# Squared lengths of the context taken from row loads for three batches, x lengths in two halves, last distance store in halves

## The chip, the cores and the metric

One core of one Trainium2 chip runs the whole program. The metric is the device time of one execution in microseconds, as the median over several runs. The engines are TensorE (PE, with its weight loads as PEld), VectorE (DVE), ScalarE (ACT), GpSimd (POOL) and SyncE (SP); DMAs are issued here by SP and ACT.

## The reference, cut to what matters

Eight batches; `x` is 100 rows of 512 numbers per batch, the context `ctx` 722 rows of 512. Four blocks follow one another, each adding to `x`: an alignment of the normalised `x` with the context by dynamic time warping, a mixture of experts, a cross attention and a second feed-forward. The change lies in the first step of the first block, the distances:

```python
aa = jnp.sum(a * a, axis=-1)[:, None]        # a: context, 722 x 512
bb = jnp.sum(b * b, axis=-1)[None, :]        # b: layernorm(x), 100 x 512
D = jnp.sqrt(jnp.maximum(aa + bb - 2.0 * (a @ b.T), 0.0))
```

The warping then walks the 722 x 100 table of D of each batch from one corner to the other and back, so it can't begin before D of all eight batches is in place (this kernel walks the eight tables at once).

## The kernel before, in words

`distances` is the first of the program's stages; `warp` follows after a barrier of all engines. Context rows are dealt to tiles by turns: tile t of the CT = 6 holds rows t, t+6, ..., so that tiles 0 and 1 have 121 rows and the others 120 (WHOLE = 120, MORE = 2, B = 8 batches, S = 100, D = 512, KD = 4, TPT = 3 tiles to a PSUM bank). For each batch b:

- SP (L171 to L182) loads the transposed context into one of four tiles `cT` (L178). From batch 4 on it first waits until the products and the squares of batch b-4 have read the buffer.
- ACT squares it, 2888 numbers per partition (`square`, L301); DVE adds the four blocks to one in two steps (`square_sums`, L239 and L243); PE multiplies the sum with a column of ones, 12 records of matmul with one column (`lengths`, L350); DVE copies the six columns into `aa` (`squares`, L248 and L249). That is `aa` of the reference.
- PE forms the products with the transposed, scaled `x`, 48 records (`products`, L339), into two PSUM banks, two pairs of which take turns.
- DVE adds products, `aa` and `bb`, three tiles after each bank (`squares`, L257); ACT takes Relu (L282) and Sqrt (L288) of all six tiles at once (`roots`).
- ACT issues the store of the distances to DRAM, a large one (L153) and a small one for the rows left over (L155); SP waits for both and loads the table back in the layout of the warping (`load_cost`, L163). `warp` waits for all eight of these loads (semaphore `c_in`), and its DVE loop (L851 to L855) starts then.

The order of the work is written out by hand. PE runs products(0), the transposes of x for batches 4 to 7, lengths(0), two small matmuls for the ranks of the mask (L365, L366), two products that spread `bb` (L370), and then for n = 1 to 7

```python
if n >= AHEAD:      # AHEAD = 6
    lengths(n)
products(n)
if n < AHEAD:
    lengths(n)
```

DVE runs square_sums(n+1) ahead of squares(n) and, after batch 0, `keep_ranks` (L134 to L149), whose positions release POOL's 48 instructions at L218. ACT runs square(n) and then roots(n-3), for n up to 10. SP issues load_cost(b-5) after the cT load of batch b, and the others at the end. The squared length of a row of normalised x (`bb`) is worked out on DVE from mean and variance after all of x (L263 to L266), for all 800 rows at once, and copied from PSUM at L271. Ahead of products(0), PE runs 10 pairs of matmuls (`keep_awake`, L81) whose result nobody reads.

Of the kernel before, what the change touches and what calls it, by code (L numbers as in the profile page):

```python
# [83 lines left out]
def distances(nc, io, res):  # L84

    ctx = ExitStack()
    with ctx:
# [9 lines left out]
        lens = res["Wmem"][0:S, B * D:B * D + B * S].rearrange("p (b s) -> p b s", s=S)  # L97
        bb = sb("bb", [P, B * S])
        NCT = 4
        cT = [sb(f"cT{i}", [P, KD, C]) for i in range(NCT)]  # L100
        cq = [sb(f"cq{i}", [P, KD, C]) for i in range(2)]
        cs = [sb(f"cs{i}", [P, C]) for i in range(2)]
        aa = sb("aa", [P, B * CT])
        d2 = sb("d2", [P, 2, CT, S])
        ds = sb("ds", [P, 2, CT, ST])
        tp = [pb(f"tpa{i}", [P, KD, P]) for i in range(2)]
        pbb = [pb(f"pbb{i}", [P, 512]) for i in range(2)]
# [11 lines left out]
        TPT, AHEAD = 3, 6  # L119
# [6 lines left out]
        prk, ptk = pbb[1][:, 400:400 + CT * B], pbb[1][:, 400 + CT * B:400 + 2 * CT * B]  # L126
# [23 lines left out]

        def store(act, b):
            act.wait_ge(ds_ok, b + 1)
            act.dma_start(res["dist"][b, 0:WHOLE * CT, :].rearrange("(p t) j -> p t j", t=CT),  # L153
                         ds[0:WHOLE, b % 2, :, :]).then_inc(ds_out[b % 2], 16)
            act.dma_start(res["dist"][b:b + 1, WHOLE * CT:C, :], ds[WHOLE:WHOLE + 1, b % 2, 0:MORE, :]).then_inc(ds_out[b % 2], 16)  # L155

        def load_cost(sp, b):

            sp.wait_ge(ds_out[b % 2], 32 * (b // 2 + 1))
            blocks = bass.AP(tensor=res["dist"].tensor, offset=b * CP * ST + PAD, ap=[[BL * ST - SK, NB], [1, BL * ST]])  # L160
            if b == 0:
                sp.wait_ge(below_out, 16)
            sp.dma_start(res["cost_mem"][b * NB:(b + 1) * NB, 0:BL * ST], blocks).then_inc(res["c_in"], 16)  # L163

        @block.sync
        def _(sp):
            for g in range(B // 2):
                sp.dma_start(x_sb[:, 2 * g:2 * g + 2, :], io["x"][2 * g:2 * g + 2].rearrange("b s d -> s b d")).then_inc(x_in[g], 16)
            sp.wait_ge(below_set, 1)
            sp.dma_start(res["dist"][:, C:CP, :].rearrange("b r s -> r b s"), below[:, :, :]).then_inc(below_out, 16)  # L170
            sp.wait_ge(m0, 1)  # L171
# [12 lines left out]
        @block.gpsimd  # L184
# [36 lines left out]
        @block.vector  # L221
        def _(dve):
            link = make_linker(dve, res["dve_chain"])
            dve.memset(d2[:, :, :, :], 0.0).then_inc(zf, 1)
            for g in range(B // 2):
                bs = slice(2 * g, 2 * g + 2)
                dve.wait_ge(x_in[g], 16)
                layernorm_stats(link, dve, x_sb[:, bs, :], stats[:, bs, :], mv[:, bs, :], 2)
                dve.tensor_scalar(rstd[:, bs], mv[:, bs, 1], EPS, None, ALU.add).then_inc(var_ok, 1)
                dve.wait_ge(st_ok, g + 1)  # L230
                link(dve.reciprocal(rstd[:, bs], rstd[:, bs]))
                for b in (2 * g, 2 * g + 1):
                    dve.tensor_scalar(xl[:, b, :], x_sb[:, b, :], mv[:, b, 0:1], rstd[:, b:b + 1],
                                      ALU.subtract, ALU.mult).then_inc(xl_ok, 1)
            def square_sums(b):

                q = cq[b % 2]
                dve.wait_ge(cq_ok, b + 1)
                dve.tensor_tensor(q[:, 0:2, :], q[:, 0:2, :], q[:, 2:4, :], ALU.add).then_inc(half_ok, 1)  # L239
                dve.wait_ge(half_ok, b + 1)  # L240
                if b >= 2:
                    dve.wait_ge(aa_mm, b - 1)
                dve.tensor_tensor(cs[b % 2][:, :], q[:, 0, :], q[:, 1, :], ALU.add).then_inc(cs_ok, 1)  # L243

            def squares(b):

                dve.wait_ge(aa_mm, b + 1)
                dve.tensor_copy(aa[0:WHOLE + 1, b * CT:b * CT + MORE], pa[b % 2][0:WHOLE + 1, 0:MORE])  # L248
                dve.tensor_copy(aa[0:WHOLE, b * CT + MORE:b * CT + CT], pa[b % 2][0:WHOLE, MORE:CT]).then_inc(aa_ok, 1)  # L249
                dve.wait_ge(aa_ok, b + 1)  # L250
# [12 lines left out]
            link(dve.tensor_tensor(length[:, :], rstd[:, :], rstd[:, :], ALU.mult))  # L263
            link(dve.scalar_tensor_tensor(length[:, :], mv[:, :, 1], float(D), length[:, :], ALU.mult, ALU.mult))
            dve.wait_ge(id1, 1)
            dve.tensor_tensor(lens[:, :, :], ident[0:S, 0:S].unsqueeze(1).broadcast_to([S, B, S]),  # L266
                              length[:, :].unsqueeze(2).broadcast_to([S, B, S]), ALU.mult).then_inc(lens_ok, 1)
            square_sums(0)
            for g in range(2):
                dve.wait_ge(bb_mm, g + 1)  # L270
                dve.tensor_copy(bb[:, g * 400:(g + 1) * 400], pbb[g][:, 0:400]).then_inc(bb_ok, 1)  # L271
            dve.wait_ge(bb_ok, 2)
            for n in range(B):
                if n + 1 < B:
                    square_sums(n + 1)
                squares(n)
                if n == 0:
                    keep_ranks(dve, link)

        def roots(act, b):  # L280
            act.wait_ge(d2_ok, 2 * b + 2)
# [10 lines left out]
        def _(act):  # L292
# [16 lines left out]
            square(0)  # L309
            for b in range(B - 4, B):  # L310
                keep_T(b)
            for n in range(1, B + 3):
                if n < B:
                    square(n)
                if n >= 3:
                    roots(act, n - 3)

        @block.tensor
        def _(pe):
# [24 lines left out]
            def lengths(b):  # L344
# [5 lines left out]
                    ins = pe.matmul(pa[b % 2][0:TR[t], t:t + 1], cs[b % 2][:, TO[t]:TO[t] + TR[t]], ones[:, 0:1], start=True, stop=True)  # L350
                ins.then_inc(aa_mm, 1)

            keep_awake(pe, pbb[0], ident, 13)
# [10 lines left out]
            pe.wait_ge(kept_ok, 1)  # L364
            pe.matmul(prk[:, :], lower[:, :], kept[:, :, :].rearrange("p t b -> p (t b)"), start=True, stop=True).then_inc(rk_ok, 1)  # L365
            pe.matmul(ptk[:, :], onesb[:, :], kept[:, :, :].rearrange("p t b -> p (t b)"), start=True, stop=True).then_inc(rk_ok, 1)  # L366
            for g in range(2):
                if g == 0:
                    pe.wait_ge(lens_ok, 1)
                pe.matmul(pbb[g][:, 0:400], ones[0:S, :], lens[:, 4 * g:4 * g + 4, :].rearrange("p b s -> p (b s)"),  # L370
                          start=True, stop=True).then_inc(bb_mm, 1)
# [2228 lines left out]
```

## Time and profile before

| | us |
|---|---|
| median of 3 runs | 1186.57 (1183.56 to 1186.99) |
| the profiled execution | 1183.51 |
| its span in the profile | 1181.6 |
| PE, DVE, ACT, POOL busy | 1065.4, 455.3, 348.5, 216.8 |
| mean granted clock of TensorE | 0.955 |

The span begins with the first instruction and ends with the last; some 1.9 us of the execution's own time lie outside it. The profiled execution is 3.1 us below the median, at the lower end of the runs. The stage of the distances takes the first 83 us. Times in the rows below are microseconds from the start of the span. Granted clock 1.00 is 2.4 GHz and 0.50 is 1.2 GHz.

### The profile page before, as it was taken

Reading aid. Unit: us, or ns where it says so; the run is one execution under the profiler, and the core shown is the slowest. Engines: PE = TensorE matmul, PEld = TensorE weight load, DVE = VectorE, ACT = ScalarE, POOL = GpSimd, SP = SyncE. Lnnn points to the kernel's source line nnn. Section 1 sums busy time; section 2 is a strip of 40 time slices with the busy share of each in tenths; the row PEclk is TensorE's granted clock in tenths of the full one; section 3 lists DMA queues with packets and bytes.
Section 4 is the critical chain, followed back from the end, with each engine's and each line's share of the span. In section 5 each row is a group of like instructions: output and inputs, shape, how many; then the busy total and the mean of one; then the engine's idle time right before and its main releaser. Section 6 shows DMA issues by size and latency. Waiting matters only on the chain. (4 is left out here: it accounts for less than half of the span.)

```text
span 1181.6 us, 17361 instructions
## 1 busy us (share of the span) xinstructions
PE 1065.4 (90%) x5421; PEld 690.2 (58%) x5422; DVE 455.3 (39%) x1694; ACT 348.5 (29%) x827; POOL 216.8 (18%) x340
## 2 busy tenths in 40 slices
PE   8956679955988999999999999989999999999997
PEld 7952235533457677777767777655456655555553
DVE  6828888883572000000000000037865553121212
ACT  4534755771021222222222222234254430000000
POOL 1853031110001111112112121210030001121211
PEclk9978799977898999999999999989999999999999
DMA  8858005117515655865595555570030005000000
GB/s 308 227 117 279 6 1 172 69 55 195 203 43 205 204 183 189 321 191 190 185 332 187 186 187 188 176 210 1 1 143 1 1 1 161 1 0 1 14 14 28
DMA packets 71802, 152.83 MB, mean 129 GB/s; under 512 B 12066, under 2 KB 16298, under 8 KB 70910
## 3 DMA queue, kind: packets, MB, share of 16 engines
q1 hardware_dynamic: 63494, 131.21, 32.7%
q0 software_dynamic: 6928, 17.04, 6.4%
q10 hardware_dynamic: 1320, 3.84, 1.2%
q8 instruction: 29, 0.48, 0.2%
q14 instruction: 31, 0.25, 0.1%
HBM read 131.83 MB, written 20.25 MB: 129 GB/s over the span
## 5 line engine op out<-in xcount | busy, mean ns | idle before, releaser
L1327 ACT ACTIVATE att<-ba,b 128x128 f32<-128x128 f32 x216 | 79.3, 367 | 308.0 <-PE ba L1297 308.0
L1347 DVE TENSOR_TENSOR att<-ba,att 128x512 f32<-128x512 f32 x27 | 18.7, 691 | 368.5 <-PE ba L1305 368.5
L1297 PEld LDWEIGHTS ba<-tiles,shared 128*128 128x128 f32 x896 | 111.5, 192 | 37.4 <-issue 37.4
L1297 PEld LDWEIGHTS ba<-tiles,Wmem 128*128 128x128 f32 x832 | 105.1, 194 | 39.3 <-issue 39.3
L1297 PE MATMUL ba<-tiles,shared 128*128 x896 | 114.4, 276 | 1.2 <-issue 0.3
L1297 PE MATMUL ba<-tiles,Wmem 128*128 x832 | 107.9, 279 | 6.0 <-issue 4.5
L1305 PE MATMUL ba<-shared,att 128*128 128x512 f32 x224 | 110.0, 593 | 0.0
L1305 PE MATMUL ba<-Wmem,att 128*128 128x512 f32 x208 | 102.2, 593 | 0.0
L2416 PE MATMUL acc<-tiles 128*128 128x400 f32 x256 | 90.6, 505 | 0.0
L2482 DVE SCALAR_TENSOR_TENSOR tiles<-bf,shared 128x400 f32<-128x400 f32 x64 | 32.4, 566 | 129.9 <-PE bf L2401 129.6
L2375 PE MATMUL bf<-shared,Wmem 128*128 128x400 f32 x192 | 70.0, 501 | 2.3 <-PEq L49 1.5
L2416 PEld LDWEIGHTS acc<-tiles 128*128 128x128 f32 x256 | 47.1, 190 | 40.4 <-issue 8.6
L1370 POOL DMA_INDIRECT sum_d<-att,to_row x27 | 43.1, 1595 | 145.3 <-DVE att L1350 145.3
L2325 POOL TENSOR_TENSOR tiles<-tiles 128x400 f32<-128x400 f32 x32 | 32.4, 1033 | 153.4 <-DVE tiles L2482 153.4
L2375 PEld LDWEIGHTS bf<-shared,Wmem 128*128 128x128 f32 x192 | 36.1, 190 | 30.1 <-issue 2.2
L2342 ACT COPY outT<-acc 128x400 f32<-128x400 f32 x4 | 1.8, 495 | 172.4 <-PE acc L2416 172.4
L887 DVE TENSOR_TENSOR_SCAN cost_mem<-reach_mem,cost_mem,enter 128x93 bf16<-128x93 bf16 x115 | 47.2, 411 | 12.1 <-DVE cost_mem L880 0.5
L1811 DVE RECIPROCAL shared<-shared 128x400 f32<-128x400 f32 x16 | 42.4, 2652 | 21.0 <-ACT shared L1711 20.8
L1521 PE MATMUL ba<-shared,Wmem 128*128 128x400 f32 x128 | 46.1, 504 | 2.6 <-DVE qT L1814 1.5
L1024 PE MATMUL px<-ctx_rows,cost_mem 128*100 128x512 f32 (+1 forms) x96 | 46.4, 626 | 0.0
L1305 PEld LDWEIGHTS ba<-shared,att 128*128 128x128 f32 x224 | 36.1, 192 | 13.4 <-issue 13.4
L855 DVE TENSOR_TENSOR_SCAN ctx_rows<-ctx_rows,cost_mem 128x46 f32<-128x46 f32 x115 | 37.4, 325 | 12.3 <-DVE ctx_rows L852 0.5
(396 smaller groups left out, 1674.7 us busy)
## 6 DMA issues: line engine op xcount, KB each, us to landing
Wmem<-in_W SPq DMA_DIRECT2D x16, 2048.0 KB, 14.1
shared<-in_W SPq DMA_DIRECT2D x16, 2048.0 KB, 12.2
cT<-in_ctxT SPq DMA_DIRECT2D x8, 1444.0 KB, 10.6
ctx_rows<-in_ctx SPq DMA_DIRECT2D x8, 1280.0 KB
Wmem<-in_Wkv SPq DMA_DIRECT2D x2, 2048.0 KB, 9.2
att<-in_b SPq DMA_DIRECT2D x16, 256.0 KB, 14.1
tiles<-in_WoT SPq DMA_DIRECT2D x4, 1024.0 KB, 13.6
Wmem<-in_WiT SPq DMA_DIRECT2D x3, 1024.0 KB, 7.1
```

The costliest lines, as they stand in the source:

```text
L855: dve.tensor_tensor_scan(reach[:, s + 1, 1:ROW], lower[:, s, :], cost[:, :, s], reach[:, s + 1, 0:1], ALU.min, ALU.add).then_inc(scanned, 1)
L887: dve.tensor_tensor_scan(walk[:, q, 1:NO], code[:, q, :], enter[:, :], walk[:, q, 0:1], ALU.mult, ALU.max).then_inc(scanned_r, 1)
L1024: ins = pe.matmul(px[b % 2][:, :], pathf[0:r, b % NPF * CT + t, :], ctx_rows[0:r, b * CT + t, :], start=t == 0, stop=t == CT - 1)
L1297: ins = pe.matmul(ph[j % NH][:, :], W1[u][:, k, j * P:(j + 1) * P], xgT[:, bass.ds(w, 1), k * P:(k + 1) * P].rearrange("p o t -> p (o t)") ...
L1305: ins = pe.matmul(py[:, :], hT[:, j - 2, :], W2[u][:, j - 2, :], start=j == 2, stop=j == HJ + 1)
L1327: act.activation(hT[:, j, :], ph[j % NH][:, :], ACT.Relu, bias=b1[:, bass.ds((e + u) * HJ + j, 1)]).then_inc(relu_ok, 1)
L1370: pool.indirect_dma_start(out=res["sum_d"], out_offset=bass.IndirectOffsetOnAxis(ap=to_row[:, 0:1], axis=0), in_=y[:, :], in_offset=None, ...
L1521: ins = pe.matmul(qk_b[j % 3][:, 0:NH2], w, lnT[:, k, g * NH2:(g + 1) * NH2], start=k == 0, stop=k == KD - 1)
L1811: link(dve.reciprocal(inv[j % 2][:, :], inv[j % 2][:, :]))
L2325: pool.tensor_tensor(hs[i % 4][:, :], h1[i % 4][:, :], h2[i % 2][:, :], ALU.add).then_inc(hs_ok, 1)
L2375: pe.matmul(bank[i % NBK][:, 0:NT4], Wi[k][:, f * P:(f + 1) * P], xT[:, k, g * NT4:(g + 1) * NT4], start=k == 0, stop=False)
L2416: ins = pe.matmul(acc[k][:, 0:NT4], WoT[:, f, k * P:(k + 1) * P], hs[i % 4][:, :], start=f == 0, stop=f == FJ - 1)
```

## The change

- Batches 5, 6 and 7 (ROWS = 5) no longer pass through `square`, `square_sums` and `lengths`. SP loads the rows of their context once more, untransposed (120 partitions with 6 rows each, and two rows over). ACT squares and sums the rows of tiles 0 to 2 (three activations with an accumulator), DVE takes mean and variance of those of tiles 3 to 5 (`bn_stats`, `bn_aggr`) and forms D times the variance plus D times the mean squared. Both write into `aa`.
- The row loads of batches 5 and 6 are issued right behind the cT loads of batches 4 and 5, that of batch 7 behind the cT load of batch 7, after a wait for square_sums(4), whose buffer it takes. load_cost(0) and (1) move behind the cT loads of batches 6 and 7.
- PE: no lengths for batches 5 to 7. `bb` of batches 0 to 3 is spread ahead of products(0), that of 4 to 7 where both were; `keep_awake` there has 4 pairs in place of 10.
- The last batch takes Relu, Sqrt and the large store in two halves of three tiles.

The core of the diff:

```diff
+        TPT, ROWS = 3, 5
-                         ds[0:WHOLE, b % 2, :, :]).then_inc(ds_out[b % 2], 16)
+            if b < B - 1:
...
+            else:
+                act.dma_start(res["dist"][b, 0:WHOLE * CT, :].rearrange("(p t) j -> p t j", t=CT)[:, TPT:CT, :],
+                              ds[0:WHOLE, b % 2, TPT:CT, :]).then_inc(ds_out[b % 2], 16)
+                return
...
+        def row_squares(sp, b):
+            sp.dma_start(rows_b[b][0:WHOLE, :, :], io["ctx"][b, 0:WHOLE * CT, :].rearrange("(p t) d -> p t d", t=CT)).then_inc(row_in[b], 16)
+            sp.dma_start(rows_b[b][WHOLE:WHOLE + 1, 0:MORE, :], io["ctx"][b:b + 1, WHOLE * CT:C, :]).then_inc(row_in[b], 16)
...
-                    sp.wait_ge(cq_ok, b - NCT + 1)
+                    sp.wait_ge(cq_ok, min(b - NCT + 1, ROWS))
                 sp.dma_start(cT[b % NCT][:, :, :], io["ctxT"][b].rearrange("(k p) c -> p k c", p=P)).then_inc(ct_in[b % NCT], 16)
-                if b > NCT:
-                    load_cost(sp, b - NCT - 1)
-            for b in range(B - NCT - 1, B):
+                if b in (NCT, NCT + 1):
+                    row_squares(sp, ROWS + b - NCT)
+                if b == B - 1:
+                    sp.wait_ge(cs_ok, ROWS)
+                    row_squares(sp, b)
+                if b >= B - 2:
+                    load_cost(sp, b - B + 2)
+            for b in range(2, B):
                 load_cost(sp, b)
...
+                if g % 2:
+                    h = slice(2 * g - 2, 2 * g + 2)
+                    link(dve.tensor_tensor(length[:, h], rstd[:, h], rstd[:, h], ALU.mult))
+                    link(dve.scalar_tensor_tensor(length[:, h], mv[:, h, 1], float(D), length[:, h], ALU.mult, ALU.mult))
...
+            def row_sums(b):
+                dve.wait_ge(row_in[b], 32)
+                for t in range(TPT):
+                    ins = dve.bn_stats(stats_r[0:WHOLE, b, t, :], rows_b[b][0:WHOLE, TPT + t, :])
+                link(ins)
+                for t in range(TPT):
+                    ins = dve.bn_aggr(mv_r[0:WHOLE, b, t, :], stats_r[0:WHOLE, b, t, :])
+                link(ins)
+                link(dve.scalar_tensor_tensor(sq_r[0:WHOLE, b, :], mv_r[0:WHOLE, b, :, 0], float(D), mv_r[0:WHOLE, b, :, 0], ALU.mult, ALU.mult))
+                dve.scalar_tensor_tensor(aa[0:WHOLE, b * CT + TPT:b * CT + CT], mv_r[0:WHOLE, b, :, 1], float(D), sq_r[0:WHOLE, b, :],
+                                         ALU.mult, ALU.add).then_inc(row_d, 1)
...
             for n in range(B):
-                if n + 1 < B:
+                if n + 1 < ROWS:
                     square_sums(n + 1)
+                elif n + 1 < B:
+                    row_sums(n + 1)
+                if n == 1:
+                    keep_lengths(1)
...
+        def last_roots(act, b):
+            for i, ts in enumerate((slice(0, TPT), slice(TPT, CT))):
+                act.wait_ge(d2_ok, 2 * b + i + 1)
+                act.activation(d2[:, b % 2, ts, :], d2[:, b % 2, ts, :], ACT.Relu).then_inc(rs_ok, 1)
+                if i == 0:
+                    act.wait_ge(ds_out[b % 2], 32 * (b // 2))
+                act.wait_ge(rs_ok, b + i + 1)
+                ins = act.activation(ds[:, b % 2, ts, PAD:ST], d2[:, b % 2, ts, :], ACT.Sqrt)
...
+            def row_sums(b):
+                act.wait_ge(row_in[b], 32)
+                for t in range(TPT):
+                    r = TR[t]
+                    ins = act.activation(rows_b[b][0:r, t, :], rows_b[b][0:r, t, :], ACT.Square,
+                                         accum_out=aa[0:r, b * CT + t:b * CT + t + 1])
+                ins.then_inc(row_a, 1)
...
             for n in range(1, B + 3):
-                if n < B:
+                if n < ROWS:
                     square(n)
-                if n >= 3:
+                elif n < B:
+                    row_sums(n)
+                if 3 <= n < B + 2:
                     roots(act, n - 3)
+            last_roots(act, B - 1)
...
-            keep_awake(pe, pbb[0], ident, 10)
+            keep_awake(pe, pbb[1], ident, 4)
+            lengths_x(0)
             products(0)
...
+            lengths_x(1)
             for n in range(1, B):
-                if n >= AHEAD:
-                    lengths(n)
                 products(n)
-                if n < AHEAD:
+                if n < ROWS:
                     lengths(n)
```

## Rows read from the trace of the kernel before

**Rows 1.** Busy times by stage: us, busy (x instructions), clock, DMA share, GB/s.

```profile
57.00:72.00 15.00, 15.00 (x128) 14.98 (x127) 7.02 (x23) 6.73 (x7) 14.17 (x22) 0.89 0.70 145
```

**Rows 2.** Timeline of PE: start, length, engine, line, out<-in, count.

```profile
23.07 3.01 PE L370 MATMUL pbb<-Wmem,ones 100*128 100x400 f32 x4
25.88 5.48 PE L339 MATMUL tpa<-xlT,cT 128*121 128x100 f32 x48
...
51.36 5.27 PE L339 MATMUL tpa<-xlT,cT 128*121 128x100 f32 x48
56.47 2.61 PE L350 MATMUL pa<-ones,cs 128*121 128x1 f32 x24
58.94 6.90 PE L339 MATMUL pd<-xlT,cT 128*121 128x100 f32 x48
...
66.88 5.27 PE L339 MATMUL tpa<-xlT,cT 128*121 128x100 f32 x48
```

**Rows 3.** The stage in slices of half a microsecond, columns as in Rows 1.

```profile
23.00:23.50 0.50, 0.50 (x5) 0.50 (x5) 0.00 (x0) 0.50 (x1) 0.00 (x0) 0.56 1.01 393
...
60.50:61.00 0.50, 0.50 (x6) 0.50 (x5) 0.00 (x0) 0.50 (x1) 0.50 (x2) 0.60 0.58 127
...
64.00:64.50 0.50, 0.50 (x6) 0.50 (x6) 0.50 (x3) 0.00 (x0) 0.50 (x1) 0.98 0.12 11
```

**Rows 4.** Timeline of the stage's head, DVE.

```profile
18.07 0.99 DVE L266 TENSOR_TENSOR Wmem<-ident,length_a 100x800 f32<-100x800 f32 x1
...
20.76 0.91 DVE L243 TENSOR_TENSOR cs<-cq 128x722 f32<-128x722 f32 x1
```

**Rows 5.** Timeline of the stage's tail and the first instruction of the warping's loop.

```profile
72.19 0.78 DVE L257 SCALAR_TENSOR_TENSOR d<-tpa,aa,bb 120x100 f32<-120x100 f32 x3 [1.64 <-PE tpa L339]
...
74.53 0.32 ACTq L153 DMA_DIRECT2D dist<-ds  x1
...
86.40 0.21 DVE L851 TENSOR_TENSOR ctx_rows<-ctx_rows 128x46 f32<-128x46 f32 x1 [2.79 <-DMA cost_mem<-dist]
```

**Rows 6.** Timeline of SP's queue: loads of the tables of batches 4, 6, 7.

```profile
67.47 0.30 SPq L163 DMA_DIRECT2D cost_mem<-dist  x1
...
74.22 0.30 SPq L163 DMA_DIRECT2D cost_mem<-dist  x1
81.74 0.30 SPq L163 DMA_DIRECT2D cost_mem<-dist  x1
```

**Rows 7.** Timeline of ACT's queue: large stores of batches 4 and 5.

```profile
63.09 0.32 ACTq L153 DMA_DIRECT2D dist<-ds  x1
...
67.54 0.34 ACTq L153 DMA_DIRECT2D dist<-ds  x1
```

**Rows 8.** Groups of ACT by form, first 170 us: count, busy us, mean ns.

```profile
L301 ACT ACTIVATE cq<-cT 128x2888 f32<-128x2888 f32 x8 | 20.7, 2606 | 15.6 <-DMA cT<-in_ctxT 9.5 <-DVE cs L243 6.1
...
L282 ACT ACTIVATE d<-d 128x600 f32<-128x600 f32 x8 | 5.5, 693 | 6.9 <-DVE d L257 6.2 <-ACT ds L288 0.7
L577 ACT ACTIVATE xg_sb<-Wmem 128x512 f32<-128x512 f32 x8 | 5.0, 623 | 0.6
...
L577 ACT ACTIVATION_READ_ACCUMULATOR xg_sb<-Wmem 128x1 f32 x8 | 1.5, 188 | 0.0
...
L305 ACT ACTIVATE rstd_a<-rstd_a 100x2 f32<-100x2 f32 x4 | 0.8, 203 | 12.0 <-DVE rstd_a L229 12.0
```

**Rows 9.** Groups of DVE by form, first 90 us.

```profile
L239 DVE TENSOR_TENSOR cq<-cq 128x1444 f32<-128x1444 f32 x8 | 13.5, 1690 | 2.2 <-ACT cq L301 2.1
...
L894 DVE BATCH_NORM_STATS2 stats_a<-x_res 100x6 f32<-100x512 f32 x8 | 5.1, 682 | 2.8 <-DMA x_res<-in_x 2.8
...
L897 DVE BATCH_NORM_AGGREGATE mv_a<-stats_a 100x2 f32<-100x6 f32 x8 | 1.0, 166 | 0.1
```

**Rows 10.** DMA issues, whole trace: count, KB each, median us to landing.

```profile
cT<-in_ctxT SPq DMA_DIRECT2D x8, 1444.0 KB, 10.6
```

**Rows 11.** Timeline of POOL: all of its 48 selections.

```profile
33.25 37.92 POOL L218 TENSOR_SCALAR Wmem<-slots_row,pos_k 128x128 bf16<-128x128 f32 x48 [17.38 <-DVE pos_k L143]
```

More of the change, by code:

```diff
@@ L99, in distances @@
         NCT = 4
+        TPT, ROWS = 3, 5
         cT = [sb(f"cT{i}", [P, KD, C]) for i in range(NCT)]
-        cq = [sb(f"cq{i}", [P, KD, C]) for i in range(2)]
+        cq_whole = sb("cq0", [P, CT * D])
+        cq = [cq_whole[:, 0:KD * C].rearrange("p (k c) -> p k c", c=C), sb("cq1", [P, KD, C])]
         cs = [sb(f"cs{i}", [P, C]) for i in range(2)]
@@ L104, in distances @@
         d2 = sb("d2", [P, 2, CT, S])
+        rows_b = {5: res["Wmem"][:, 5 * KD * D // 2:5 * KD * D // 2 + CT * D], 6: sb("rows6", [P, CT * D])[:, :], 7: cq_whole[:, :]}
+        rows_b = {b: t.rearrange("p (t d) -> p t d", d=D) for b, t in rows_b.items()}
+        stats_r, mv_r, sq_r = sb("stats_r", [P, B, TPT, 6]), sb("mv_r", [P, B, TPT, 2]), sb("sq_r", [P, B, TPT])
+        row_in, row_a, row_d, half_ds = [sem(f"row_in{b}") for b in range(B)], sem("row_a"), sem("row_d"), sem("half_ds")
         ds = sb("ds", [P, 2, CT, ST])
@@ L125, in distances @@
         flag, one8, runs, pos = sb("flag", [P, B]), sb("one8", [P, B]), sb("runs", [P, B]), res["pos"]
-        prk, ptk = pbb[1][:, 400:400 + CT * B], pbb[1][:, 400 + CT * B:400 + 2 * CT * B]
+        prk, ptk = pbb[0][:, 400:400 + CT * B], pbb[0][:, 400 + CT * B:400 + 2 * CT * B]
         sel, slots_row = res["sel"], sb("slots_row", [P, KC])
@@ L152, in store @@
             act.wait_ge(ds_ok, b + 1)
-            act.dma_start(res["dist"][b, 0:WHOLE * CT, :].rearrange("(p t) j -> p t j", t=CT),
-                         ds[0:WHOLE, b % 2, :, :]).then_inc(ds_out[b % 2], 16)
+            if b < B - 1:
+                act.dma_start(res["dist"][b, 0:WHOLE * CT, :].rearrange("(p t) j -> p t j", t=CT),
+                              ds[0:WHOLE, b % 2, :, :]).then_inc(ds_out[b % 2], 16)
+            else:
+                act.dma_start(res["dist"][b, 0:WHOLE * CT, :].rearrange("(p t) j -> p t j", t=CT)[:, TPT:CT, :],
+                              ds[0:WHOLE, b % 2, TPT:CT, :]).then_inc(ds_out[b % 2], 16)
+                return
             act.dma_start(res["dist"][b:b + 1, WHOLE * CT:C, :], ds[WHOLE:WHOLE + 1, b % 2, 0:MORE, :]).then_inc(ds_out[b % 2], 16)
         def load_cost(sp, b):
-            sp.wait_ge(ds_out[b % 2], 32 * (b // 2 + 1))
+            sp.wait_ge(ds_out[b % 2], 32 * (b // 2 + 1) + (16 if b == B - 1 else 0))
             blocks = bass.AP(tensor=res["dist"].tensor, offset=b * CP * ST + PAD, ap=[[BL * ST - SK, NB], [1, BL * ST]])
@@ L234, in _ @@
                                       ALU.subtract, ALU.mult).then_inc(xl_ok, 1)
+                if g % 2:
+                    h = slice(2 * g - 2, 2 * g + 2)
+                    link(dve.tensor_tensor(length[:, h], rstd[:, h], rstd[:, h], ALU.mult))
+                    link(dve.scalar_tensor_tensor(length[:, h], mv[:, h, 1], float(D), length[:, h], ALU.mult, ALU.mult))
+                    dve.wait_ge(id1, 1)
+                    dve.tensor_tensor(lens[:, h, :], ident[0:S, 0:S].unsqueeze(1).broadcast_to([S, B // 2, S]),
+                                      length[:, h].unsqueeze(2).broadcast_to([S, B // 2, S]), ALU.mult).then_inc(lens_ok, 1)
             def square_sums(b):
@@ L243, in square_sums @@
                 dve.tensor_tensor(cs[b % 2][:, :], q[:, 0, :], q[:, 1, :], ALU.add).then_inc(cs_ok, 1)
-            def squares(b):
[L247 to L250, printed above, removed]
+            def row_sums(b):
[9 more added lines that the diff above has]
+                                         ALU.mult, ALU.add).then_inc(row_d, 1)
+            def squares(b):
+                if b < ROWS:
+                    dve.wait_ge(aa_mm, b + 1)
+                    dve.tensor_copy(aa[0:WHOLE + 1, b * CT:b * CT + MORE], pa[b % 2][0:WHOLE + 1, 0:MORE])
+                    dve.tensor_copy(aa[0:WHOLE, b * CT + MORE:b * CT + CT], pa[b % 2][0:WHOLE, MORE:CT]).then_inc(aa_ok, 1)
+                    dve.wait_ge(aa_ok, b + 1)
+                else:
+                    dve.wait_ge(row_d, b - ROWS + 1)
+                    dve.wait_ge(row_a, b - ROWS + 1)
                 if b >= 2:
@@ L261, in squares, with keep_lengths @@
                         ins.then_inc(d2_ok, 1)
[L263 to L267, printed above, removed]
             square_sums(0)
-            for g in range(2):
+            def keep_lengths(g):
                 dve.wait_ge(bb_mm, g + 1)
                 dve.tensor_copy(bb[:, g * 400:(g + 1) * 400], pbb[g][:, 0:400]).then_inc(bb_ok, 1)
-            dve.wait_ge(bb_ok, 2)
+            keep_lengths(0)
+            dve.wait_ge(bb_ok, 1)
             for n in range(B):
-                if n + 1 < B:
+                if n + 1 < ROWS:
                     square_sums(n + 1)
+                elif n + 1 < B:
+                    row_sums(n + 1)
+                if n == 1:
+                    keep_lengths(1)
+                if n == B // 2:
+                    dve.wait_ge(bb_ok, 2)
                 squares(n)
@@ L278, in _ @@
                     keep_ranks(dve, link)
+        def last_roots(act, b):
[6 more added lines that the diff above has]
+                ins = act.activation(ds[:, b % 2, ts, PAD:ST], d2[:, b % 2, ts, :], ACT.Sqrt)
+                if i == 0:
+                    ins.then_inc(half_ds, 1)
+                    act.wait_ge(half_ds, 1)
+                    act.dma_start(res["dist"][b, 0:WHOLE * CT, :].rearrange("(p t) j -> p t j", t=CT)[:, 0:TPT, :],
+                                  ds[0:WHOLE, b % 2, 0:TPT, :]).then_inc(ds_out[b % 2], 16)
+                    act.dma_start(res["dist"][b:b + 1, WHOLE * CT:C, :],
+                                  ds[WHOLE:WHOLE + 1, b % 2, 0:MORE, :]).then_inc(ds_out[b % 2], 16)
+            ins.then_inc(ds_ok, 1)
+            store(act, b)
         def roots(act, b):
@@ L351, in lengths, with lengths_x @@
                 ins.then_inc(aa_mm, 1)
+            def lengths_x(g):
+                pe.wait_ge(lens_ok, g + 1)
+                pe.matmul(pbb[g][:, 0:400], ones[0:S, :], lens[:, 4 * g:4 * g + 4, :].rearrange("p b s -> p (b s)"),
+                          start=True, stop=True).then_inc(bb_mm, 1)
             keep_awake(pe, pbb[0], ident, 13)
@@ L364, in _ @@
             pe.wait_ge(kept_ok, 1)
+            pe.wait_ge(bb_ok, 1)
             pe.matmul(prk[:, :], lower[:, :], kept[:, :, :].rearrange("p t b -> p (t b)"), start=True, stop=True).then_inc(rk_ok, 1)
             pe.matmul(ptk[:, :], onesb[:, :], kept[:, :, :].rearrange("p t b -> p (t b)"), start=True, stop=True).then_inc(rk_ok, 1)
[L367 to L371, printed above, removed]
+            lengths_x(1)
             for n in range(1, B):
-                if n >= AHEAD:
-                    lengths(n)
                 products(n)
-                if n < AHEAD:
+                if n < ROWS:
                     lengths(n)
```

1 line of the change is left out of this document (removed).

## The prediction

> **What bounds the kernel now.** I looked first at the busy times by stage. In the second half of the distances PE is busy all 15 us of 15, DVE and ACT less than half, and the DMA engines 0.70 of the time [rows 1]. The timeline of PE says what it does there: products and lengths follow each other without a gap from 25.88 us on, the last product ends at about 72.15 [rows 2], and behind it comes a short serial tail: last sums on DVE, Relu and Sqrt, store, load, first instruction of the warping's loop at 86.40, which the trace puts down to the DMA into cost_mem [rows 5]. What follows hangs on that DMA alone: the loop runs over all batches at once, and SP, POOL and PE start their share of `warp` from the same barrier. So a microsecond taken from the distances is a microsecond of the whole, unless the barrier holds it. The slices of half a microsecond add one thing: the granted clock falls to 1.2 GHz twice while PE is busy, once from 23.0 us, shortly after the lengths of batch 0, and once from 60.5 to 64.0, with 2.47 us of one-column lengths of batches 5 and 6 just before [rows 2, 3].
>
> **PE between 51.36 and 72.15.** The stretch is 20.79 us and holds products(5), lengths(5) and (6), products(6), lengths(7), products(7). Start to start a product takes 56.47 - 51.36 = 5.11, two lengths take 58.94 - 56.47 = 2.47, so one takes 1.23, and products(6) takes 66.88 - 58.94 - 1.23 = 6.71, 1.6 more than its neighbour, because it lies in the slow clock [rows 2, 3]. After the change three products remain, 3 x 5.11 + 0.16 for the end of the last = 15.5. Lengths give 3.7, and the slow stretch 1.6 if it goes with the run of small matmuls ahead of it, which I take to be so because the single lengths of batches 1 to 4 had no fall behind them. Gain 5.3; bounds 3.7 (the clock falls all the same) and 5.3.
>
> **The head.** The halved spread of `bb` takes two of four records out from between lengths(0) and products(1): at 3.01 us for four, 1.5 [rows 2]. Against it, the first half of the x lengths (a half of 0.99 and two small operations of some 0.17, together 0.85 us, [rows 4]) now stands ahead of the last two groups of x on DVE; ACT's square(0) stands behind the last of these, so the sum of squares, ready at 21.67 [rows 4], comes at about 22.5 and PE, which takes it at 21.80, waits some 0.7. The slow clock after 23.0 moves with it and would cover about 1.5 us more of products(1), costing 0.75 [rows 3]. Net between a loss of 0.5 and a gain of 1.5; I take 0.3 gained. The spread for batches 0 to 3 before products(0) takes the place of six pairs of keep_awake while PE waits for the first context; nothing.
>
> **ACT and DVE for batches 5 to 7.** ACT gives up one square of 2.61 and gets three activations of 0.62 with 0.19 for each accumulator, 2.4 [rows 8]. DVE gives up 1.69 and 0.91 and two copies, and gets three bn_stats of 0.68, three bn_aggr of 0.17 and two small operations of some 0.17, 2.9 [rows 4, 9]. Per batch both stay under 5 us beside a product of 5.11: hidden by PE. DVE is the nearer one: 2.9 and six sums of some 0.3, 4.8 in all. If that cover went it would cost a few tenths a batch.
>
> **The row loads.** Each is as large as a cT load, 1.47 MB, 3.7 us at the 393 GB/s of a full slice [rows 3]; three are 11 us of full DMA. SP issues those of batches 5 and 6 behind cT loads and so pushes cT(5) and cT(6) back by about 4 us, and all stores of that time share the engines. Who waits: products(6) wants its cT at about 56, and before it was there at about 49. The rows of batch 7 can be issued once the sum of squares of batch 4 is done, at about 45, and by the median landing of 10.6 us of a cT load [rows 10] they are there at 56. Behind their wait stand roots(4) on ACT and, on DVE, squares(6), which can't end before products(6) does at 61. Slack 3 to 5 us: nothing in the sum. load_cost(0) and (1) behind later loads delay nobody, as c_in counts all eight.
>
> **The tail.** Today 72.97 (end of DVE) to 74.53 (issue of the store) is 1.56 [rows 5]. Relu of 600 numbers takes 0.69 and an activation of two takes 0.20 [rows 8], so one of 300 takes 0.45; two of them and the gaps are 1.05: gain 0.5. From the store's issue at 74.53 to SP's load at 81.74 it is 7.2 [rows 5, 6]. For batch 4 the same step took 67.47 - 63.09 = 4.4 [rows 6, 7]. The difference is that batch 7's store had the load of batch 6 (74.22) in front of it, on the same DMA engines. After the change only a half of the bytes is left for the last store. Bounds: 3.3 (batch 4's step without about 1 us of data) and 7.2; I take 4.5, since the load of batch 6 will still be issued at about that time: gain 2.7. The load itself, 81.74 to 86.34 or so, stays at 4.6; if it follows batch 6's load closely it could lose 1.
>
> The Trainium skill, DMA: Bandwidth & Descriptors, Anatomy of one DMA, speaks against this term: a DMA costs about 2.0 us whatever its size and moves the rest at 436 GB/s, so halving 331 KB saves 0.4. This case's store needs far more than its 2.8 us, so the trace does not agree on the size; it agrees that most of a store isn't data.
>
> **Sum.** 5.3 + 0.3 + 0.5 + 2.7 = 8.8 us. The profiled execution took 1183.51, so it would take 1174.7; the median of the runs is 3.06 higher, 1186.57, and I forecast from it: **1177.8**. POOL's selections run to 71.17 [rows 11] and begin when batch 0's sums are done, 1 us or so earlier than now; SP's last load would be issued at about 73, so POOL doesn't become the barrier's last, but by 2 us only.
>
> **Rivals.** (a) The store gains nothing: what it waits for is the load of batch 6 and the fixed part of a DMA, not its bytes. Then 7.2 stays (or 0.4 goes), the gain is 6.1 to 6.5, and the time 1180.3. For: batch 5's store, issued 0.07 us after batch 4's load, needed 6 us until SP passed it; against: batch 4's 4.4. (b) The clock falls in the last batches or at the head all the same: PE's gain is 3.7 and the head's none, 6.9 in all, time 1179.7. For: it fell at 60.5 with PE busy throughout, some 2 us into products; against: no fall between 27 and 60. (c) DMA or DVE becomes the bound of batches 5 to 7: the queue of cT and row loads runs late by some 5 us beyond the slack, gain 0 to 4, time about 1184.5. (d) Slower: rows of batch 7 hold ACT. They stand behind cT(7) on SP's queue, and roots(4) stands behind them on ACT; each microsecond past about 58 goes to the end, and from 58 + 8.8, about 67, on the kernel is slower than before. A landing at 70 would make 1190. Against: it would take 25 us for a load whose median is 10.6 [rows 10].
>
> **Chances.** Forecast 0.62, (a) 0.16, (b) 0.12, (c) 0.07, (d) 0.03. The forecast's own range from its bounds is 1174.5 to 1180.5. With (a) and (b), and with the 3.4 us over which the three runs of before spread, it becomes 1173.5 to 1182.5. About 0.3%, 3.6 us, is what a measurement of this kernel can tell from no change. Faster by more than that is the forecast, (a) and (b), 0.90; within it most of (c), 0.07; slower 0.03.
>
> **What would show it.** Right: PE's products of batches 5, 6 and 7 back to back, 5.1 apart, the last ending at about 66.5; no slice at 0.50 after 30 us; DVE and ACT with row operations that end before the product they belong to; the last store issued at about 68, SP's last load at 72 to 73, the loop's first instruction at 77 to 78. Wrong: idle DVE at L257 put down to ACT or to a DMA before the last products; ACT waiting at the row sums of batch 7 beyond 58; 7 us between the last store and the load; DVE idle put down to POOL at the barrier; or anything after the barrier that isn't simply shifted.

## The result and the profile after

The changed kernel is slower: median 1199.3 us of six runs (1193.18 to 1202.57) against 1182.44 of the kernel before in the same series, ratio 1.0137 with a 95% interval of 1.0112 to 1.0162. The profiled execution took 1201.74 us, span 1200.1. The forecast was 1177.8, with a range of 1173.5 to 1182.5.

The timeline of PE in the changed kernel, start and length in us:

```profile
51.62 5.27 PE L415 MATMUL tpa<-xlT,cT 128*121 128x100 f32 x48
64.00 7.52 PE L415 MATMUL pd<-xlT,cT 128*121 128x100 f32 x48 [7.10 <-DMA cT<-in_ctxT]
73.85 6.92 PE L415 MATMUL tpa<-xlT,cT 128*121 128x100 f32 x48 [2.33 <-DMA cT<-in_ctxT]
```

Up to products(5), at 51.62, PE stands where it stood before [rows 2]. The lengths behind it are gone as planned, but then PE has nothing to work on: the context of batches 6 and 7 isn't there until 64.0 and 73.85. Both also take longer than the 5.27 us of products(5): in the first the granted clock was 0.50 up to 66 us, after PE had stood idle. The waits between 50 and 92 us, longest first, say that PE isn't even the worst placed (engine, line, what it waited for: total, times, longest):

```profile
ACT cq L381 <- DMA cq<-in_ctx: 21.7, 1, 21.7
DVE stats_r L276 <- DMA cq<-in_ctx: 20.0, 1, 20.0
ACT rows L381 <- DMA rows<-in_ctx: 12.0, 1, 12.0
PEld pd L415 <- DMA cT<-in_ctxT: 7.3, 1, 7.3
PE pd L415 <- DMA cT<-in_ctxT: 7.1, 1, 7.1
```

ACT and DVE wait for the rows of batch 7 (`cq<-in_ctx`) 21.7 and 20.0 us. The timelines of SP and ACT give issue and use of the three row loads (the tile of batch 5's rows is called `Wmem`, that of batch 6's `rows`):

```profile
20.96 0.51 SPq L177 DMA_DIRECT2D Wmem<-in_ctx  x1
...
32.09 0.50 SPq L177 DMA_DIRECT2D rows<-in_ctx  x1
...
44.73 5.40 SPq L177 DMA_DIRECT2D cq<-in_ctx  x1
```

```profile
42.50 0.63 ACT L381 ACTIVATE Wmem<-Wmem 121x512 f32<-121x512 f32 x1 [2.79 <-DMA Wmem<-in_ctx]
...
57.88 0.63 ACT L381 ACTIVATE rows<-rows 121x512 f32<-121x512 f32 x1 [12.04 <-DMA rows<-in_ctx]
...
82.91 0.63 ACT L381 ACTIVATE cq<-cq 121x512 f32<-121x512 f32 x1 [21.69 <-DMA cq<-in_ctx]
```

They need 21.5, 25.8 and 38.2 us from issue to use, where a cT load before had a median of 10.6 from issue to landing [rows 10]; ACT stood waiting at each, so use and landing are the same here. The issue of the third held SP itself for 5.40 us. Behind the last load the stage's end is a queue of work that was held back: roots(4) to (6) come one right after another from 84.8 on, and

```profile
98.20 0.32 ACTq L162 DMA_DIRECT2D dist<-ds  x1
...
106.19 0.21 DVE L928 TENSOR_TENSOR ctx_rows<-ctx_rows 128x46 f32<-128x46 f32 x1 [4.01 <-DMA cost_mem<-dist]
```

the last store goes out at 98.20 (74.53 before) and the warping's loop starts at 106.19 (86.40 before, [rows 5]). The loop starts 19.8 us later and the profiled execution is 18.2 us longer, so the whole loss lies ahead of the loop; what follows it took 1.6 us less than before, which is inside the spread given below. Between 20 and 60 us the DMA engines are busy all the time and move hardly more, first before, then after (columns as in Rows 1):

```profile
20.00:60.00 40.00, 39.66 (x357) 38.15 (x355) 30.81 (x83) 23.38 (x19) 26.75 (x32) 0.96 0.81 251
```

```profile
20.00:60.00 40.00, 36.34 (x325) 35.20 (x324) 29.42 (x85) 19.99 (x27) 27.86 (x40) 0.96 1.02 274
```

At 0.81 busy they moved 251 GB/s, at 1.02 only 274. Per busy share that is 310 before and 269 after: the engines are not just asked for more, they are slower at it.

### The profile page after: what moved, and what is told of

It reads as the page before. It is cut to its first block and busy times, and to the rows that moved or that the text cites. A ratio compares the mean times of both kernels' runs of the same rounds, so it can differ in the third digit from the quotient of the medians.

```text
span 1200.1 us, 17300 instructions
## 1 busy us (share of the span) xinstructions
PE 1063.5 (89%) x5373; PEld 687.7 (57%) x5374; DVE 454.7 (38%) x1709; ACT 347.1 (29%) x844; POOL 211.3 (18%) x340
## 5 line engine op out<-in xcount | busy, mean ns | idle before, releaser
L1382 PEld LDWEIGHTS ba<-shared,att 128*128 128x128 f32 x224 | 36.1, 192 | 13.4 <-issue 13.4
## 6 DMA issues: line engine op xcount, KB each, us to landing
cT<-in_ctxT SPq DMA_DIRECT2D x8, 1444.0 KB, 16.1
```

Source lines behind the costliest of these rows:

```text
L1382: ins = pe.matmul(py[:, :], hT[:, j - 2, :], W2[u][:, j - 2, :], start=j == 2, stop=j == HJ + 1)
```

## The experiments

How to read the times: ratios are to the kernel before on the same chips. In the twelve profiled executions (both kernels and all runs but the two of single DMAs), the execution's time less the loop's start lay between 1092.8 and 1102.2 us, though the program behind the loop's start is the same in all. What makes this spread wasn't tested. So a single execution tells what happened in the stage, by the loop's start, and only the ratio tells the kernel's time. Experiments 5 and 10 rest on one execution each.

**1. Long runs, or the quantity?** e1_short_runs:

```diff
+        RD = D + 8
-        cq_whole = sb("cq0", [P, CT * D])
+        cq_whole = sb("cq0", [P, CT * RD])
...
-        rows_b = {b: t.rearrange("p (t d) -> p t d", d=D) for b, t in rows_b.items()}
+        rows_b = {b: t.rearrange("p (t d) -> p t d", d=RD)[:, :, 0:D] for b, t in rows_b.items()}
```

> The changed kernel, with each row of 512 numbers of the row loads landing 8 numbers apart from the next, so that a load moves runs of 2048 B in place of one run of 12288 B per partition; nothing else differs. Theory L (long runs): the packets of 12288 B took about 1.0 us each where one of 2888 B takes 0.12, so the loads ran at half the rate; with short runs they go at some 400 GB/s, rows of batches 5, 6, 7 are there by 33, 41 and 56 us, PE's last product ends at about 66.5 and the time is 8 us under the kernel before. Theory Q (quantity): 4.4 MB more in the same queue is what holds everything, whatever the runs; cT of batch 7 lands beyond 70 us and the time stays 15 us above the kernel before.

Measured: ratio 1.0101 (1.0061 to 1.0141), rows of batch 7 used at 81.73, loop at 104.78. Packets between 31 and 34 us, first in the changed kernel, then here:

```profile
DMA packets 55, 0.54 MB, mean 181 GB/s; under 512 B 0, under 2 KB 0, under 8 KB 14
## 3 DMA queue, kind: packets, MB, share of 16 engines
q1 hardware_dynamic: 55, 0.54, 92.5%
```

```profile
DMA packets 273, 0.57 MB, mean 190 GB/s; under 512 B 1, under 2 KB 1, under 8 KB 273
## 3 DMA queue, kind: packets, MB, share of 16 engines
q1 hardware_dynamic: 273, 0.57, 101.5%
```

The packets did become short, and the rate only went from 181 to 190 GB/s, with the engines busy all the time. My first theory falls: the length of the runs is not it. Theory Q stands so far.

**2. Is it the row path at all?** e2_no_rows puts all batches back on the old path (`ROWS = 8`, no row_squares, the old orders of PE and SP) and keeps the rest of the change.

> The changed kernel without its row path: all eight batches squared and summed as before, in PE's and SP's old order; the two halves of the x lengths, the shorter keep_awake and the halved last store stay. Theories L and Q alike: the loss is gone. By the terms of the prediction the head gives 0.3, the halved tail 0.5 and the halved store 2.7, so 3.5 us under the kernel before; if the store's halving gives nothing, 0 to 1 us under.

Measured: 0.9987 (0.9966 to 1.0007), loop at 82.12. The loss sits in the row path. What the rest brings, some 1.5 us where I expected 3.5, its interval doesn't separate from nothing.

**3. The loads alone.** e3_loads_only adds to the kernel before

```diff
+                if b in (NCT, NCT + 1):
+                    row_squares(sp, 5 + b - NCT)
...
+            for b in (5, 6):
+                sp.wait_ge(row_in[b], 32)
```

> The kernel before, plus the row loads of batches 5 and 6 in the changed kernel's places on SP, with load_cost(0) and (1) moved behind as there; nobody reads what they load. Both theories: the loads alone, without any of the new work on ACT and DVE, make cT of batches 6 and 7 late. L: each load holds the engines some 8 us, so cT(7) lands at about 65 to 70 in place of 59 and the time is 0 to 5 us over the kernel before. A third theory W (the waits for rows on ACT and DVE, not the engines' share): cT lands as before and the time is the same as before within 1 us.

Measured: 1.0081 (1.0044 to 1.0118), loop at 97.50. Two loads that nobody reads cost 10 us. ACT in its timeline:

```profile
49.61 2.61 ACT L313 ACTIVATE cq<-cT 128x2888 f32<-128x2888 f32 x1 [9.59 <-DMA cT<-in_ctxT]
63.62 2.61 ACT L313 ACTIVATE cq<-cT 128x2888 f32<-128x2888 f32 x1 [10.01 <-DMA cT<-in_ctxT]
72.36 2.61 ACT L313 ACTIVATE cq<-cT 128x2888 f32<-128x2888 f32 x1 [4.74 <-DMA cT<-in_ctxT]
```

cT(6) and cT(7) are squared at 63.6 and 72.4, 14 and 13 us later than before, more than either theory gave. Theory W falls: without any new work on ACT or DVE, the two loads alone take the DMA engines' time from the cT loads behind them.

**4. The last store whole again.** e4_short_whole_store is e1_short_runs with the old `roots` and `store` for batch 7.

> As e1_short_runs, with Relu, Sqrt and store of the last batch whole, as before. By the prediction's terms it is 3.2 us slower than e1_short_runs (0.5 of ACT, 2.7 of the store); by the rival that a store's time is not its bytes, 0.5 to 1 us slower.

Measured: 1.0132 (1.0081 to 1.0182), median 1200.58 against 1196.56, loop at 106.05 against 104.78. The loop starts 1.3 us later and the medians are 4.0 us apart, but the intervals overlap: whether it is 0.5 to 1 us or 3.2 stays undecided here.

**5. Each load by itself.** With length and company both in doubt I measured the loads alone, behind the last load_cost, SP waiting for each (one function for each form, in this pattern):

```diff
+                sp.dma_start(rows6[0:128, :, :], every[3610:3610 + 768, :].rearrange("(p t) d -> p t d", t=6)).then_inc(alone[1], 16)
+                sp.wait_ge(alone[1], 16)
```

> The kernel before with eight loads of some 1.4 MB at the end of the distances, one after the other on SP, each waited for before the next is issued, nothing else in the DMA queues: (1) the row load of the change, 120 partitions by 12288 B; (2) the same with 128 partitions; (3) with 112; (4) 120 partitions by six runs of 2048 B that lie 120 rows apart; (5) the same with 128 partitions; (6) a cT load, 128 by four runs of 2888 B; (7) 112 partitions and 8 partitions in two loads; (8) as (1) again. Theory N (number of partitions): (1), (4) and (8) take about 8 us and (2), (3), (5), (6), (7) about 5.5, since 120 partitions are dealt to the DMA engines badly. Theory S (source): long stretches of DRAM read by one partition are slow, (1), (2), (3), (7), (8) take about 8 us and (4), (5), (6) about 5.5. Theory M (mixture): alone all take about 5.5 us, and it is only in company with cT loads and stores that the row loads are slow.

SP's timeline has it in the distances between the issues:

```profile
83.14 0.34 SPq L190 DMA_DIRECT2D rows<-in_ctx  x1
92.43 0.36 SPq L194 DMA_DIRECT2D rows<-in_ctx  x1
98.98 0.31 SPq L198 DMA_DIRECT2D rows<-in_ctx  x1
106.04 0.34 SPq L202 DMA_DIRECT2D rows<-in_ctx  x1
115.77 0.39 SPq L206 DMA_DIRECT2D rows<-in_ctx  x1
122.77 0.39 SPq L210 DMA_DIRECT2D rows<-in_ctxT  x1
128.98 0.33 SPq L214 DMA_DIRECT2D rows<-in_ctx  x1
```

120 partitions 9.3 us, 128 partitions 6.6 with 7% more bytes, 112 partitions 7.1, 120 with short scattered runs 9.7, 128 with the same 7.0, the cT load 6.2, and 112 and 8 in two loads 8.3 (137.25 less 128.98; 137.25 is the next row in the trace). So it is the number of partitions, whatever runs and source look like: theories S and M fall. N is right on 120 against 128, though all loads take about 1 us more than it said, and 112 partitions, which it had among the fast ones, take longer than 128 for fewer bytes. Load (8) has no issue behind it to go by; 120 partitions take 9.3 us again in experiment 10. Packets in the middle of load (1) and of load (2), stretches of 3 and 2 us:

```profile
DMA packets 55, 0.68 MB, mean 225 GB/s; under 512 B 0, under 2 KB 0, under 8 KB 0
## 3 DMA queue, kind: packets, MB, share of 16 engines
q1 hardware_dynamic: 55, 0.68, 94.2%
```

```profile
DMA packets 66, 0.81 MB, mean 406 GB/s; under 512 B 0, under 2 KB 0, under 8 KB 0
## 3 DMA queue, kind: packets, MB, share of 16 engines
q1 hardware_dynamic: 66, 0.81, 97.0%
```

A packet of the same 12288 B holds an engine 0.942 x 16 x 3 / 55 = 0.82 us in the first and 0.970 x 16 x 2 / 66 = 0.47 us in the second. This is an estimate, as packets are cut at the edges of so short a stretch.

**6. The change with faster row loads.** e6_rows_128 reads 128 partitions for batches 5 and 6, and 112, 8 and 1 for batch 7:

```diff
+            if b < B - 1:
+                sp.dma_start(rows_b[b][:, :, :], every[b * C:b * C + P * CT, :].rearrange("(p t) d -> p t d", t=CT)).then_inc(row_in[b], 16)
+                return
```

> The changed kernel with its row loads dealt to another number of partitions: batches 5 and 6 read 128 partitions by 6 rows (46 rows past the batch's end land in partitions that nobody reads; the two rows over come with them), batch 7 reads 112 and 8 partitions. Theory N (120 partitions go at half rate, found with the loads alone): the row loads take 4 us of the engines in place of 8, rows of batches 5, 6, 7 are there by 36, 46 and 60 us, cT(7) by 56, PE has no gap of over 1 us before its last product, which ends by 68, and the time is 5 to 8 us under the kernel before. Theory Q (quantity, 4.4 MB more): cT(7) lands beyond 66 and the time is above the kernel before's.

Measured: 1.0042 (1.0021 to 1.0064), loop at 88.42. Of the 1.37% lost, 0.42% is left, and PE works back to back as predicted:

```profile
52.64 5.27 PE L420 MATMUL tpa<-xlT,cT 128*121 128x100 f32 x48
57.75 5.22 PE L420 MATMUL pd<-xlT,cT 128*121 128x100 f32 x48
62.80 5.22 PE L420 MATMUL tpa<-xlT,cT 128*121 128x100 f32 x48
```

Its last product ends at 68.0. The rows of batches 5 and 6 are used at 39.45 and 45.63. But ACT still waits 15.6 us for the rows of batch 7, until 65.41, with roots(4) behind it, and the time is above the kernel before's and not 5 to 8 us under it. N is right about the rate, and not the whole of it.

**7. The unused loads with 128 partitions.** e7_loads_only_128 is e3_loads_only with the DMA of experiment 6.

> As e3_loads_only, the kernel before with two row loads that nobody reads, but with 128 partitions each. N: cT(6) is squared on ACT from about 53 in place of 63.6 and cT(7) from about 60 in place of 72.4 (49 and 59 in the kernel before), and of the 10 us that e3_loads_only lost less than 3 are left. Q: the loss stays within 2 us of e3_loads_only's.

Measured: 1.0012 (0.9989 to 1.0035), loop at 82.62, cT(6) and cT(7) squared at 49.6 and 57.3:

```profile
49.58 2.61 ACT L313 ACTIVATE cq<-cT 128x2888 f32<-128x2888 f32 x1 [4.63 <-DMA cT<-in_ctxT]
57.28 2.61 ACT L313 ACTIVATE cq<-cT 128x2888 f32<-128x2888 f32 x1 [3.70 <-DMA cT<-in_ctxT]
```

The same two loads that cost 10 us with 120 partitions cost nothing that can be measured with 128; theory Q falls for two loads. One more thing differs in this pair: with 120 partitions the two rows over need a small load of their own each. Experiment 5 has no such loads and shows the same slow rate, so the number of partitions is the cause in both.

**8, 9. Two batches by rows.** e8_two_by_rows puts batch 7 back on the old path, lengths(7) ahead of products(7); e9_small_store_last also moves the store of the rows over behind the second half.

> As e6_rows_128, with batch 7 back on the old path (square, sums, lengths ahead of its products), so that two row loads of 128 partitions are left. Theory NQ (both the number of partitions and, for the third load, a queue that is full to 66 us): nothing waits for a DMA any more; PE's last product ends at about 69 and the loop of the warping starts at 80 to 82, 4 to 6 us under the kernel before. Theory H (it is not the queue but the odd split of batch 7's load in 112, 8 and 1 partitions that made it late): the same, so this run does not tell these two apart, but if ACT or DVE still wait here, both fall. If the kernel stays at e6_rows_128's time, the row path itself costs more than the lengths it takes from PE.

> As e8_two_by_rows, with the last batch's store of the rows over issued behind the second large half. In the traces so far ACT stood 2.0 to 2.5 us in the issue of that small store before it could go on with the second half. If that stop comes from the small store itself, the second half goes out up to 2 us earlier and the loop starts 0 to 1 us earlier (the small store then lands last); if it comes from the large store in front of it, still being turned into descriptors, the stop moves to the second half's large store and nothing is gained.

Measured: 0.9992 (0.9968 to 1.0017) and 0.9989 (0.9967 to 1.0012): level with before. In the profiled executions the loop starts at 88.23 (in e8's slowest execution, 1190.4 us) and 86.26, since ACT waits 12.6 and 12.2 us for cT(7), to 63.3 and 60.6; I had expected no wait for a DMA, so by the expectation's own words NQ and H both fall for this kernel. In the loads without readers (experiment 7) cT(7) was there at 57.3; why it is later here wasn't tested. The old path needs cT(7) earlier than the row path, and its square stands on ACT ahead of roots(4). Of the small store: e8's profile has ACT in its issue for only 0.28 us, so there was nothing to win; moved, it takes 0.99 us, and the second half waited for DVE. The stop isn't bound to this store: ACT stood 2.47 us in it in the changed kernel, 2.38 in e2_no_rows and 2.21 in e11_all_128, but 0.28 in e1_short_runs and e6_rows_128, where the large second half took 1.33 and 1.39 us to issue in its place. No gain is shown, and what makes the stop stays open.

**10. More DMAs by themselves.** e10_more_alone, as experiment 5.

> The kernel before with single DMAs at the end of the distances, each waited for before the next: loads of 64, 60, 96, 104 and 120 partitions by 12288 B, then stores of the distances of 120, 112, 128 and 120 partitions by 2760 B runs. Theory K (the partitions are dealt in equal shares to the largest number of engines up to 16 that divides them, so 16, 15, 16, 13, 15, and anything but 16 is slow): 60 partitions take as long as 96 or longer, 104 take longer than 112 took (7.1 us), 120 again 9.3 us; the store of 120 takes 1 us or more longer than that of 128. Theory P (15 or 13 engines, each at full rate): 60, 104 and 120 partitions take within 10% of what 64, 112 and 128 take.

Loads of 64, 60, 96, 104 and 120 partitions took 5.9, 5.9, 7.1, 9.0 and 9.3 us; stores of 120, 112 and 128 took 2.8, 2.7 and 2.7. Neither theory: 104 and 120 are slow, as K has it, but 64, which 16 divides, takes 5.9 us for half the bytes of 128, and 96 takes as long as 112. Three microseconds of the load of 64:

```profile
DMA packets 62, 0.76 MB, mean 254 GB/s; under 512 B 0, under 2 KB 0, under 8 KB 0
q1 hardware_dynamic: 62, 0.76, 107.4%
```

That is 0.83 us a packet. Worked out in the same way a packet takes 0.80 us with 60 partitions, 0.79 with 96, 0.82 with 104, 0.63 with 112 and 0.47 with 128. A full 128 is the only fast one among those measured. The stores of this kernel don't suffer.

**11. All three with 128.** e11_all_128 replaces batch 7's three loads by one of 128 partitions that ends with the tensor, so batch 7's squared lengths are those of other rows.

> As e6_rows_128, with batch 7's row load in one DMA of 128 partitions too; so that it stays inside the tensor it reads the last 768 rows of the context, which are not the rows that belong in those partitions, so the squared lengths of batch 7 are of other rows. This is the prediction's own case, every row load at the full rate. Theory Q (the queue is full to the end): rows of batch 7 are there no earlier than 62 us (65.4 with the split load), ACT still waits over 10 us for them, and the time is at best level with the kernel before. Theory H (the split load): they are there by 58, ACT and DVE wait under 2 us beyond the slack, and the time is 6 to 9 us under the kernel before, as predicted.

Measured: 1.0022 (1.0002 to 1.0042), loop at 86.89. The rows are used at 63.85 in place of 65.41; the wait on ACT is still 15.3 us. Its stretch from 20 to 60 us:

```profile
20.00:60.00 40.00, 39.48 (x357) 38.62 (x357) 31.23 (x93) 21.23 (x28) 27.99 (x40) 0.96 1.03 365
```

365 GB/s in place of 274, and busy to the end. Theory H falls, Q holds for the third load: issued behind cT(7) at 44.54 us, it had no room before 60 us with 128 partitions either. Whether it would have fitted at another place in the queue wasn't tried.

**12. One batch by rows.** e12_one_by_rows keeps batch 5 alone on the row path.

> The changed kernel with only batch 5 by rows, loaded with 128 partitions, and batches 6 and 7 on the old path with their lengths ahead of their products; load_cost in its old places. One more load of 1.5 MB falls into the stretch in which the DMA engines of the kernel before stand still (28 to 33 us). Theory NQ: cT(6) and cT(7) land within 2 us of before (49.4 and 59.1), nothing waits for the rows, PE saves one set of lengths (1.2 us) over e2_no_rows, the last product ends at about 69.7, the loop starts at 81 to 82, and the time is 3 to 6 us under the kernel before. If even one more load makes cT(7) late, the loop starts at 84 or later and the row path has no place here at all.

Measured: 1.0020 (0.9996 to 1.0045), though the profiled execution, at 1174.67, was the fastest of twelve that reach to 1190.59; in it the loop started at 80.56 and cT(7) was squared at 57.9. It shows the stage as NQ has it once, with the loop's start 5.8 us earlier, and no gain on the whole. What spreads its runs wasn't tried; their list does show that the longer executions have the lower mean granted clock, 0.961 at 1174.67 us and 0.955 at 1190.59, and the same in e8_two_by_rows, 0.965 at 1173.81 and 0.952 at 1190.4. Which comes of which isn't shown. No version here beats the kernel before by more than the measurement can tell.

## Why the prediction was wrong

**The step that failed** is the one on the row loads: "Each is as large as a cT load, 1.47 MB, 3.7 us at the 393 GB/s of a full slice". It took the price of a load from its bytes and the rate from a load of another shape. With 120 partitions the row load ran at 225 GB/s alone and at 181 GB/s in company, which makes 6.5 to 8.1 us of the engines for its 1.47 MB, and 20 to 24 us for three of them where the sum had 11 (experiments 1, 5, 7). So cT(6) was not pushed back by about 4 us but by 15, from 49.4 to 64.0. A second mistake stands in the same part: "by the median landing of 10.6 us of a cT load [rows 10] they are there at 56". That median belongs to a queue that empties between loads (0.24 busy from 28 to 33 us, 0.81 from 20 to 60); with three more loads it never does, and even with 128 partitions the rows come at 63.9 (experiment 11). "Slack 3 to 5 us: nothing in the sum" fell with these two.

**Point by point.**
- Rival (d), given 0.03, is what happened. Its price, slack to 58 and rows at 82.9, so 24.9 less the gain of 8.8, gives 16.1 over the profiled 1183.5, 1199.6; measured 1201.7. That it comes so near is in part luck: by the same working the loop would start at 77.6 + 24.9 = 102.5 and it started at 106.19, since roots(4) to (6) stood in a queue behind the rows, which the price didn't have, while the rest of the program happened to be 1.6 us shorter. The path was right and the chance was read off the wrong number. The wait for cT, rival (c), came with it.
- PE between 51.36 and the end: 5.1 us a product without lengths, right wherever data was there (experiments 6, 11). The 1.6 us of slow clock was put down to the two lengths in a row. e2_no_rows and e7_loads_only_128 have the same 2.6 us of them (e7 with the kernel before's whole order on PE) and products(6) behind takes 5.27 in both, not 6.90. So the two lengths don't bring the fall by themselves, and its 1.6 us can't be counted as a gain of the change; what brought it in the one execution stays open. The line of e7_loads_only_128:

```profile
59.13 5.27 PE L351 MATMUL pd<-xlT,cT 128*121 128x100 f32 x48
```

- The head: forecast +0.3, though its own terms (1.5 less 0.7 less 0.75) add up to 0.05. In e2_no_rows the start of products(2) moved from 32.41 to 32.73. PE waits 0.78 us for the sums, as said, and products(1) takes 6.25 in place of 5.48, in the slow clock. A loss of 0.3, inside the bounds, on the wrong side.
- The tail: 3.2 forecast, and in e2_no_rows the way from DVE's last sum to the loop is 82.12 - 71.67 = 10.5 against 13.4, so 3.0. That the sum fits is luck, as the parts were mis-sized and the errors cancel: the half store needs 2.5 us until SP's load where I had 4.5; DVE's end to the last store's issue takes 2.4 where I had 1.05, because ACT loses 2.4 in the issue of the small store, which I had not priced; and the last load to the loop takes 5.6 us in place of 4.7. ACT's timeline in e2_no_rows:

```profile
70.31 0.32 ACTq L333 DMA_DIRECT2D dist<-ds  x1
70.67 2.38 ACTq L335 DMA_DIRECT2D dist<-ds  x1
...
73.09 0.45 ACT L325 ACTIVATE d<-d 128x300 f32<-128x300 f32 x1 [2.81 <-issue]
...
74.06 0.32 ACTq L162 DMA_DIRECT2D dist<-ds  x1
```

- Against the Trainium skill, DMA: Bandwidth & Descriptors, Anatomy of one DMA, I wrote that this store needs far more than 2.8 us. That figure is an estimate from the page's 2.0 us and 436 GB/s, which it gives for DMAs issued by GpSimd. Alone in the queue, issued by SP, the store takes 2.8 (experiment 10), so the trace agrees. The other 4.4 us of the kernel before I put down to waiting behind the loads of batches 5 and 6, issued at 73.62 and 74.22 just ahead of it; no run takes these loads away by themselves, so this is argued and not shown.
- ACT's and DVE's row operations cost no more than was said: for batch 7 in the changed kernel 1.95 us (forecast 2.4) and 2.6 us (2.9) from first to last. Their waits were the bound, not their work.

## What to carry to other kernels

Price a new DMA by a load of its own shape, partitions first, and not by bytes and the rate of another; where the trace has none, run it alone once. Then add it to the DMA engines' busy time of the stretch in which it must land: engines at 0.81 busy have room for about a fifth more, and a load that doesn't fit makes loads behind it late. Here two loads of 128 partitions fitted in experiment 7, with cT(7) used at 57.3; in experiments 8 and 9 it was 3 to 6 us later, and a third load did not fit (experiment 11). Spreading a load over all 128 partitions, with rows that nobody needs, can be faster than moving only what is needed: 6.6 us against 9.3.

## What was not expected of the hardware

- A load of 120 partitions moves 225 GB/s where one of 128 moves 406, and takes 9.3 us against 6.6; with runs of 2048 B it is 9.7 against 7.0. All loads measured with fewer than 128 partitions have slower packets of 12288 B, an estimated 0.63 us (112) to 0.83 us (64) against 0.47. The Trainium skill, DMA: Bandwidth & Descriptors, Why a DMA increments its semaphore by 16 and not by 1, has a DMA use the largest number of engines up to 16 that divides its outer sizes, 15 for 120 partitions. The trace agrees, with a busy share of 0.942 of 16; but 15 of 16 explains 6% and not that each packet takes 0.82 us for 0.47. Why the packets are slower stays open. Stores to DRAM with 120 partitions showed nothing of it.
- ACT can stand in the issue of a store of 0.9 KB for 2.4 us, right behind the issue of a large one, and for 0.28 us in another run; SP stood 5.40 us in the issue of the third row load in the changed kernel and 0.60 in e11_all_128.
- The clock's fall under a busy PE is not tied to the same instructions from one execution to the next: from 61 to 62 us the granted clock is 0.50 in the kernel before and 1.00 in e7_loads_only_128, with PE busy and in the same order in both.
